# Selective-state block, group 0: VectorE masks the two decay tiles before the convolution taps of the next group's first x tile

## What is computed

```python
proj = hidden_states @ in_proj_w.T          # 128 tokens
gate, hBC, dt = split(proj)                 # 8192, 8192 + 2 * 8 * 128, 128
hBC = silu(conv1d_4_taps(hBC) + conv_b)     # causal, one filter a channel
x, Bm, Cm = split(hBC)                      # x: 128 heads of 64; B, C: 8 groups of 128
dt = softplus(dt + dt_bias)
A_dt = -exp(A_log) * dt
Lmat = exp(segment_sum(A_dt))               # per head, 128 x 128, lower triangle
Gm = C @ B.T                                # per group, 128 x 128
M = Gm * Lmat
y = M @ (x * dt) + D * x
y = y * rsqrt(mean(y * y) + EPS) * norm_w * silu(gate)
out = y @ out_proj_w.T
```

## Time and profile before

| | |
|---|---|
| median of 3 runs | 699.57 us (699.56 to 699.96) |
| the profiled execution, its own time | 698.99 us |
| its span | 697.3 us |
| PE busy | 671.9 us, 96% of the span |
| DVE busy | 436.9 us, 63% |
| ACT busy | 356.7 us, 51% |
| POOL busy | 117.1 us, 17% |
| TensorE clock granted, mean | 0.988 of full speed |

### The profile page before, as it was taken

One profiled execution on the slowest core, in us unless ns is written; L12 is line 12 of the kernel. 1 busy time (PEld: TensorE's weight loads), 2 busy tenths in 40 slices (PEclk: granted clock), 3 DMA queues, 4 the chain that ended last, 5 costly groups with the idle time before them and its releaser, 6 DMA issues.

```text
span 697.3 us, 12695 instructions
## 1 busy us (share of the span) xinstructions
PE 671.9 (96%) x4450; PEld 575.4 (83%) x4450; DVE 436.9 (63%) x1095; ACT 356.7 (51%) x706; POOL 117.1 (17%) x75
## 2 busy tenths in 40 slices
PE   7999998999999999999999987997999999999897
PEld 6888887899999999999999977996797797796453
DVE  2533115767777777677677765779857757756562
ACT  4403116667776677678766652664435435434101
POOL 0000001112431143114321133022220220200100
PEclk9999999999999999999999999998999999999989
DMA  8511001011021110311031503953577667647702
GB/s 257 240 61 60 1 1 61 1 56 67 1 71 52 64 56 0 120 60 60 0 111 50 240 12 145 293 199 144 203 242 264 223 238 274 214 175 276 283 20 98
DMA packets 15701, 87.07 MB, mean 125 GB/s; under 512 B 3584, under 2 KB 3968, under 8 KB 6064
## 3 DMA queue, kind: packets, MB, share of 16 engines
q1 hardware_dynamic: 15088, 85.52, 34.0%
q10 hardware_dynamic: 576, 1.05, 0.5%
HBM read 86.30 MB, written 0.26 MB: 124 GB/s over the span
## 4 chain that ended last, share of the span: by engine, by line
PE 92%; DVE 4%; ACT 2%; DMA 1%; issue 1%; SPq 0%; DVEq 0%; ACTq 0%
PE ps L1284 18%; PE ps L1079 15%; PE ps L1080 15%; PE ps L1081 14%; PE ps L1191 8%; PE ps L1324 8%; PE ps L1148 4%; PE ps L1313 2%; PE ps L1396 2%; PE ps L1431 2%; DMA ring<-wk_dram 1%; PE ps L1295 1%; PE ps L1304 1%; PE ps L1296 1%; DVE acc L922 1%; ACT prob L524 1%
## 5 line engine op out<-in xcount | busy, mean ns | idle before, releaser
L711 DVE TENSOR_TENSOR pt_lo<-ps,pt_hi 128x512 fp32r<-128x512 f32 x144 | 95.1, 661 | 72.0 <-ACT pt_hi L442 71.1
L1284 PEld LDWEIGHTS ps<-norm_t,ring 128*128 128x128 f32 x1152 | 132.6, 193 | 4.8 <-issue 3.9
L1284 PE MATMUL ps<-norm_t,ring 128*128 128x128 f32 x1152 | 133.8, 276 | 0.0
L442 ACT ACTIVATE pt_hi<-ps 128x512 fp32r<-128x512 f32 x144 | 82.2, 571 | 85.0 <-PE ps L1191 84.7
L524 ACT ACTIVATE prob<-prob,neg_max 128x512 f32<-128x512 f32 (+1 forms) x128 | 94.6, 741 | 7.5 <-DVE neg_max L803 7.5
L922 DVE SCALAR_TENSOR_TENSOR acc<-raw,cw,acc 128x127 f32<-128x127 f32 (+2 forms) x240 | 78.5, 402 | 27.9 <-ACT acc L622 27.9
L799 DVE TENSOR_SCALAR_CACHE_REDUCE prob<-ps 128x512 f32<-128x512 f32 (+1 forms) x160 | 92.0, 605 | 2.6 <-PE ps L1081 1.2
L1079 PE MATMUL ps<-pt_hi,v_hi 128*128 128x256 f32 x272 | 88.3, 325 | 0.0
L1191 PE MATMUL ps<-ident,prob 128*128 128x128 f32 x544 | 83.2, 273 | 1.9 <-DVE pt_lo L711 1.3
L1191 PEld LDWEIGHTS ps<-ident,prob 128*128 128x128 f32 x544 | 65.2, 140 | 14.9 <-DVE pt_lo L711 2.2
L1080 PE MATMUL ps<-pt_hi,v_lo 128*128 128x256 f32 x272 | 76.4, 281 | 0.0
(11 more groups left out here) (170 smaller groups left out, 1097.6 us busy)
## 6 DMA issues: line engine op xcount, KB each, us to landing
ring<-w_in_dram SPq DMA_DIRECT2D x36, 1024.0 KB, 4.8
ring<-w_out_dram SPq DMA_DIRECT2D x16, 1024.0 KB, 4.8
ring<-wq_dram SPq DMA_DIRECT2D x8, 1024.0 KB, 5.9
ring<-wo_dram SPq DMA_DIRECT2D x8, 1024.0 KB, 4.8
ring<-w_dram SPq DMA_DIRECT2D x4, 896.0 KB, 6.0
ring<-ctx_t_dram SPq DMA_DIRECT2D x3, 1024.0 KB, 6.8
ring<-w_dram SPq DMA_DIRECT2D x3, 1024.0 KB, 4.7
ring<-wk_dram SPq DMA_DIRECT2D x4, 256.0 KB, 8.2
```

The costliest lines, as they stand in the source:

```text
L442: copy = lambda dst, src: nc.scalar.activation(dst, src, ACT.Copy)
L711: sub = lambda dst, a, hi: nc.vector.tensor_tensor(dst, a, hi, ALU.subtract)
L1284: ins = mm(ps[:, bank, t * T:t * T + T], w[:, t, c, :], norm_t[:, c, :], start=(c == 0), stop=(c == NC - 1))
```

## The change

VectorE's program ahead of the loop is written in another order. Behind the mask of the gates (`gm`, L979), `mask_decay(0, 0, 0)` and `mask_decay(0, 0, 1)` now come first, and the taps of the first x tile of group 1 behind them.

```diff
             nc.vector.tensor_tensor(gm[:], ps[:, 6:8, :].rearrange("p a (g t) -> p (a g) t", t=T),
                                     causal[:].unsqueeze(1).to_broadcast([P, GROUPS, T]),
                                     ALU.mult).then_inc(gm_ok, 1)
-            taps_of(8, 6, 0, 8)
             dve.wait_ge(gm_ok, 1)
             mask_decay(0, 0, 0)
             mask_decay(0, 0, 1)
+            taps_of(8, 6, 0, 8)
             taps_of(9, 7, 1, 12)
             mask_decay(1, 1, 0)
             skip_add(0, 0)
```

## The result

| | before | after |
|---|---|---|
| median, 14 runs of each side by side | 699.72 us (697.01 to 700.81) | 701.95 us (700.35 to 703.26) |
| ratio after to before | | 1.0034 (95%: 1.0024 to 1.0045) |
| span of the profiled execution | 697.3 us | 700.2 us |

The account below looks back on a forecast made before the run. TensorE, 96% busy, was taken as the bound. Its 5.9 us gain was given back plus 0.4; with 2.8 of slow clock, 3.2 on 698.99 made 702.2, and 0.58 to the median 702.8 us, range 699.8 to 703.8.

Parts of the forecast that it names:

- Step 1: VectorE ahead of the loop: the second decay mask ends at 471.86 instead of 475.18, worth 3.3 us there.
- Step 2: TensorE around group 0: y products start at 472.03 at full clock, a gain of 5.9 us on this engine.
- Steps 3 and 4: POOL's selects for group 2 start at 475.17, under VectorE's second taps, and hold them up by 3.6 us.
- Step 5: TensorE idles 6.8 us for skip_add and resumes at 485.45 instead of 485.06: the gain given back, 0.4 us more.
- Step 6: TensorE behind the new wait: half clock for 5.5 us in the first loop step, losing 2.8 us (1.7 to 3.4).
- Step 7: Behind the slow stretch: the first loop step's y products don't wait, and all 3.2 us pass to the end.
- Rival A: VectorE's second taps: POOL doesn't hold them up, TensorE resumes 3.2 us earlier, 696.4 or 698.1 to 699.8 us; chance 0.13.
- Rival B: TensorE's clock: slow stretch short (1.7 us lost), last stretch gives 1.7 us back, no change at 700.0 us; chance 0.12.
- Rival C: First mask loses to both POOL instructions, y products begin no earlier than 472.2, change does nothing; no share.

Follow-up runs that it names:

- pool_short: The changed kernel with POOL's two selects for group 2 writing one head's columns instead of sixteen: 698.74 us, ratio 0.9979 to the kernel before.
- the filled kernel: The changed kernel with 28 idle products on TensorE behind project(0, 3), in its wait: 700.63 us, ratio 1.0008 to the kernel before.
- The filled kernels: Idle products in TensorE's wait: 28 in the changed kernel, 700.63 us, and 18 in the kernel before, 697.25 us.
- ahead: The changed kernel with skip_add directly behind the first taps and project(1, 0) ahead of the first loop step's transposes: 697.03 us, ratio 0.9971 to the kernel before.

## Why the prediction was right, and where its size was off

The forecast was slower by 3.2 us; 2.2 were measured, within its range.

- *Step 1, the masks.* Right. POOL's second select takes 2.99 us, as forecast from the one row that showed this position, and the second mask ends 1.07 us behind it, at 471.84 on the old scale (forecast 471.86).
- *Step 2, TensorE.* Right to 0.1 us: y products at 472.00 (forecast 472.03), at full clock. The gain of 5.9 us on this engine was there (POOL's pair starts at 475.18, against 481.07).
- *Steps 3 and 4, the collision.* Right. 3.6 us were forecast on the second taps; they took 6.86 us to the next instruction (476.81 to 483.67) where 3.36 are undisturbed, so 3.5. `pool_short` takes 3.3 us out of T. The other reckoning, that VectorE loses the selects' whole 2.00 + 2.05 us, is 0.5 too high.
- *Step 5, the new wait.* Right. Transposes at 485.40 on the old scale (forecast 485.45), 6.71 us of idle time (6.8), released by `skip_add`, as the wait for yv says.
- *Step 6, the clock.* The term that was mis-sized. It was taken at 2.8 us, the half of 5.5. After TensorE resumed, the slow stretches lasted 3.2 and 5.3 us in two profiles and cost 1.5 and 2.5 us of Y - T against the filled kernel; between the medians it is 1.6. So the half was right and the length wrong: a part of the stretch falls into the wait and costs nothing, and how large that part is differs between executions. I had taken one profile's stretch as the typical one. The lower bound I gave, 1.7, was already above the cheaper of the two. It came from a stretch that I misread: that one doesn't count from when TensorE resumed at 421.38, since the four transposes there still took 0.66 us against 1.11 at 661.81, and the slow clock began 1.4 us later. My own range of 701.5 to 703.8 should have begun at 701.3 by its terms.
- *Step 7, behind it.* Right in that the y products of step 1 don't wait and that all passes to the end. But the 6.71 us from the earlier trace rows held 0.28 us of waiting for POOL's second tile, and the change takes them away. So of the 0.34 us in T only 0.06 are left in Y, and nearly all of the forecast's sum is the slow clock: 0.06 + 1.5 = 1.6 and, in the other profile, 0.1 + 2.5 = 2.6 us of Y. The 2.2 us between the medians lie between them. The filled kernels give the same loss another way: the new order costs 2.7 us of Y, and the clock costs 1.4 or 2.4 us where it cost 2.6 before. The last slow stretch is nearly as long as before (6.79 us in the earlier trace rows):

```profile
664.50:671.10 6.60, 5.33 (x16) 3.76 (x17) 0.90 (x3) 0.87 (x2) 0.00 (x0) 0.50 0.24 102
```

Rival A has fallen. POOL arrived in a stream of taps, which no row had shown, and its first select took 2.13 us, 0.13 more than undisturbed: it waited for one tap, not for the stream. Rival B's two accidents didn't meet. Its clock term was nearer to the truth than mine, but the last stretch gave nothing back. Rival C has no share either: the first mask got in between POOL's two selects.

## What to carry to other kernels

Before an instruction is moved up, follow what it releases on the engines off the critical path: here an earlier product freed POOL 5.9 us sooner, under VectorE's second taps, which its selects hold up, and the whole gain was given back there. A stall that is moved keeps its second price if TensorE's clock falls in the new wait too. What it costs is the part of the slow stretch that lies behind the wait, and one profile doesn't say how long that is; the same work of TensorE's own put into the wait, with its PSUM bank's last reader looked up first, gave the lowest median of the versions that compute all (697.03 us).

## What had not been expected of the hardware

- The clock fell between 489.2 and 489.3 behind idle times of 0.67 and 1.75 us that ended 3.8 us apart (`ahead`). In the kernel after, an idle time of 1.59 us by itself, at 471.03, was not followed by a fall.
- Executions of one kernel differ by where and for how long the clock falls. The changed kernel's two profiles were 1.05 us apart in Y, 0.03 of it in T. The 12 runs of `ahead` were 8.7 us apart in time, and their mean granted clocks go the same way, from 0.998 in the fastest to 0.980 in the slowest.
